# Local attention: one semaphore for the even and one for the odd slots' value transfers

## The reference, cut to what matters

```python
for i in range(DEPTH):            # 6
    x = attn_layer(shift_tokens(x), Wqkv[i], q_scale[i], k_scale[i], Wo[i]) + x
    x = ffn_layer(shift_tokens(x), ln_g[i], ln_b[i], W1[i], b1[i], W2[i], b2[i]) + x
```

```python
bk2, bv2 = (look(bk), look(bv))   # each window with the one before
sim = jnp.einsum('bhwie,bhwje->bhwij', bq, bk2) * QK_SCALE
attn = jax.nn.softmax(jnp.where(mask, -jnp.finfo(sim.dtype).max, sim), -1)
out = jnp.einsum('bhwij,bhwje->bhwie', attn, bv2)
```

## Time and profile before

| what | value |
|---|---|
| three runs | 2665.85, 2668.93, 2667.49 us |
| median | 2667.49 us |
| profiled execution | 2667.58 us |
| its span, first to last instruction | 2665.8 us |
| mean granted TensorE clock | 0.971 of full |
| PE / DVE / ACT / POOL busy | 2491.4 / 2005.2 / 1888.8 / 1764.4 us |
| local stage, first to last attention product | 630.8 to 2309.7 us |

### The profile page before, as it was taken

How to read it: one execution, slowest core, us unless ns; L and a number is a source line. 1 busy time by engine, 2 the same in 40 slices (tenths; PEclk the granted TensorE clock), 3 DMA queues, 4 the chain that set the end, 5 groups by cost and what they waited for, 6 DMA issues and landing times.

```text
span 2665.8 us, 98075 instructions
## 1 busy us (share of the span) xinstructions
PE 2491.4 (93%) x36437; PEld 1732.2 (65%) x36441; DVE 2005.2 (75%) x4387; ACT 1888.8 (71%) x6630; POOL 1764.4 (66%) x1605
## 2 busy tenths in 40 slices
PE   6999788987899999999999999999999999789999
PEld 5888444444666666666666666666666666458884
DVE  5555576766688888888888888888888888565544
ACT  4777666755788888888888878888888888543323
POOL 1777755537788887887888888888887888312210
PEclk9999888888999999999999999999999999989999
DMA  4000100002111211121111111111112111100000
GB/s 117 14 14 15 47 10 9 10 8 80 29 32 35 63 38 35 33 57 40 40 34 52 47 39 33 47 50 42 33 33 64 42 33 33 38 1 1 1 1 16
DMA packets 176292, 91.06 MB, mean 34 GB/s; under 512 B 40926, under 2 KB 172232, under 8 KB 175824
## 3 DMA queue, kind: packets, MB, share of 16 engines
q1 hardware_dynamic: 167200, 80.50, 11.2%
q0 software_dynamic: 8192, 4.21, 1.1%
q10 hardware_dynamic: 432, 0.07, 0.0%
HBM read 30.57 MB, written 3.76 MB: 13 GB/s over the span
## 4 chain that ended last, share of the span: by engine, by line
PE 27%; DMA 23%; SPq 19%; issue 3%; DVE 2%; ACT 0%; DVEq 0%
DMA rg_prod<-vt 22%; SPq L556 18%; PE bank L1119 3%; PE bank L1136 2%; PE scores L1171 2%; PE bank L1182 2%; PE bank L1126 2%; PE scores L1153 1%; PE bank L1852 1%; PE bank L1876 1%; PE bank L2109 1%; PE bank L1846 1%; PE bank L1870 1%; PE bank L1211 1%; PE bank L1108 1%
## 5 line engine op out<-in xcount | busy, mean ns | idle before, releaser
L1554 POOL TENSOR_TENSOR rs<-ssc,neg_half 128x8 f32<-128x8 f32 x384 | 647.2, 1685 | 40.8 <-DVE ssc L1375 40.7
L1482 ACT ACTIVATE pr<-scores,negmax 128x64 f32<-128x64 f32 x1536 | 461.8, 313 | 58.5 <-DVE negmax L1383 32.8
L1544 POOL TENSOR_TENSOR t_pair<-qn_pair,tabs 128x512 f32<-128x512 f32 x384 | 489.1, 1274 | 13.9 <-DVE qn_pair L1363 13.1
L1534 POOL TENSOR_TENSOR pr<-pr,rec 128x256 f32<-128x256 f32 x384 | 235.7, 614 | 305.4 <-DVE rec L1355 304.9
L1119 PE MATMUL bank<-wqk,xs 128*128 128x512 f32 x768 | 405.1, 610 | 22.0 <-DVE qn_pair L1363 19.3
L1013 POOL DMA_INDIRECT rg_win<-rg_images,share_down x256 | 253.6, 991 | 144.4 <-DVE rg_prod L952 89.9
L1482 ACT ACTIVATION_READ_ACCUMULATOR pr<-scores,negmax 128x1 f32 x1536 | 311.6, 203 | 0.0
L1371 DVE TENSOR_REDUCE ss<-sq 128x8 f32<-128x512 f32 x384 | 261.4, 681 | 30.9 <-ACT sq L1505 29.8
L1363 DVE TENSOR_TENSOR qn_pair<-bank,rs 128x512 f32<-128x512 f32 x384 | 258.2, 672 | 29.8 <-POOL rs L1554 29.6
L1473 ACT COPY vt<-bank 128x256 f32<-128x256 f32 x361 | 135.2, 375 | 203.9 <-issue 116.7
L1136 PE MATMUL bank<-oT,wo 128*128 128x128 f32 x1536 | 266.4, 296 | 0.0
(11 more groups left out here) (307 smaller groups left out, 5596.0 us busy)
## 6 DMA issues: line engine op xcount, KB each, us to landing
rg_prod<-vt SPq DMA_DIRECT2D x1536, 32.0 KB
wqk<-in_L_ffn_Wqkv SPq DMA_DIRECT2D x20, 256.0 KB
rg_win<-rg_images,share_down POOLq DMA_INDIRECT x256
wv<-in_L_ffn_Wqkv SPq DMA_DIRECT2D x20, 128.0 KB
wo<-in_L_ffn_Wo SPq DMA_DIRECT2D x20, 128.0 KB
w<-in_L_ffn_W SPq DMA_DIRECT2D x6, 341.0 KB
rg_images<-rg_prod SPq DMA_DIRECT2D x1, 1625.0 KB, 8.0
rg_images<-XT SPq DMA_DIRECT2D x16, 64.0 KB
```

Source lines behind the costliest of these rows:

```text
L1482: ex = act.activation(pr[t % 2][:, h * BAND:(h + 1) * BAND], sl_ps[:, h // 2, h % 2 * BAND:(h % 2 + 1) * BAND], ACT.Exp, bias=negmax[t % 2 ...
L1544: pool.tensor_tensor(t2[t % 2][:, :].rearrange("p (i h f e) -> p i h f e", i=2, h=GH, f=2), qn[t % 2][:, :].rearrange("p (i h f e) -> p i ...
L1554: pool.tensor_tensor(rs[t % 2][:, :], ssc[t % 2][:, :], neg_half[:, 0:8], ALU.pow)\
```

## The change

The single semaphore becomes two. The transfers of even jobs raise the first, those of odd jobs the second. SP's wait at L554 asks for the transfers of job t-2 and is left out for the first two jobs. PE asks for this job's own, by the parity's count. The two copies ask for job t-3's, by that job's parity; ACT has no such wait for the first three jobs. Nothing else is touched.

```diff
-        self.v_spread = sem("attn_v_spread")
+        self.v_spread = [sem(f"attn_v_spread{i}") for i in range(2)]
...
                     sp.wait_ge(a.o_ready, TICKS + t - 1)
-                    if t:
-                        sp.wait_ge(a.v_spread, 64 * t)
+                    if t >= 2:
+                        sp.wait_ge(a.v_spread[t % 2], 64 * (t // 2))
                     for to, half, key, a_pair in ((0, 0, WINDOW, 0), (0, 1, HD, 0), (HD, 0, WINDOW, 1), (HD, 1, 0, 1)):
                         sp.dma_start(far[to:to + HD, half * P:(half + 1) * P],
-                                     near[key:key + BAND, a_pair * P:(a_pair + 1) * P]).then_inc(a.v_spread, 16)
+                                     near[key:key + BAND, a_pair * P:(a_pair + 1) * P]).then_inc(a.v_spread[t % 2], 16)
...
                 pe.wait_ge(a.pT_moved, TICKS + t + 1)
-                pe.wait_ge(a.v_spread, 64 * (t + 1))
+                pe.wait_ge(a.v_spread[t % 2], 64 * (t // 2 + 1))
...
                     dve.wait_ge(a.o_ready, TICKS + t - 2)
-                    dve.wait_ge(a.v_spread, 64 * (t - 2))
+                    dve.wait_ge(a.v_spread[(t - 3) % 2], 64 * ((t - 3) // 2 + 1))
...
                     act.wait_ge(a.o_ready, TICKS + t - 2)
-                    act.wait_ge(a.v_spread, 64 * max(t - 2, 0))
+                    if t >= 3:
+                        act.wait_ge(a.v_spread[(t - 3) % 2], 64 * ((t - 3) // 2 + 1))
```

## The result

| | before | changed |
|---|---|---|
| runs | 2665.85, 2668.93, 2667.49, 2661.22 us | 2644.14, 2636.15, 2639.70, 2642.06 us |
| median | 2666.67 us | 2640.88 us |
| profiled execution, its span | 2667.58, 2665.8 us | 2644.14, 2642.3 us |

The ratio is 0.9913, with a 95% interval of 0.9893 to 0.9933: by the ratio 23 us faster, somewhere between 18 and 29; the medians differ by 25.8. The forecast was 2648.5 us, in a range of 2644.0 to 2658.0. The profiled execution of the changed kernel, 2644.14 us, is the slowest of its four and lies 3.3 us above their median; that of before lies 0.9 above its own. So the two profiles differ by 23.4 us and not by 25.8.

The account below looks back on a forecast made before the run. The prediction took SP's transfer turn, about as slow as TensorE's slot, to bound the local stage. Its terms, 19.1 + 1.6 - 3.9 + 2.5 = 19.3 us, and a count by cycles led to 19.0: 2648.5 us, range 2644 to 2658.

Parts of the forecast that it names:

- Two things at nearly the same pace, and a queue that can't make up what it loses: Local stage: SP's transfer turn averages about 4.3 us against a TensorE slot of 4.31 to 4.38, so attention is held.
- The part by part costs: Waits on PE, DVE and ACT cost nothing; SP's value copy is long done, transfers lead attention by 3 to 4.5 us.
- Given back, 3.9 us: TensorE's waits before the scores, after ACT's three Gelus per chunk, grow from 17.2 to 21.1 us over 22 chunks.
- The last slots, 0.9 and 2.5 us: Stage end: 0.9 us gained for two held slots behind 2253.27, 2.5 us for the last two slots.
- By cycles, 13.1 to 17.5 us: Second count, 19 chunk cycles from 925.00 to 2253.27 us: an excess of 17.5, or 13.1 if 4.4 stay.
- first rival: The ring of engines sets the slot, so stalls return: half back 2658 us, chance 0.12; all back 2663.4.
- the 19.1 us: TensorE's stalls before attention, 750 to 2290 us: 16.2 us idle plus 2.9 for overlap with the scores' bar.
- the first term of the sum: TensorE's idle time before attention from 750 to 2290 us, 16.2 us for 49 held slots, is gained.
- Rival 4: More is gained: nothing of the 3.9 us before the scores comes back, 2644.4 us; chance 0.03.
- my 19.0: Whole kernel: forecast gain of 19.0 us, taken between the two counts, from 2667.5 to 2648.5 us.
- Stalls passed on to other engines: Local stage: other engines needed the rest held attentions gave; half back 2658 us, chance 0.12, all back 2663.4.
- Transfers queuing behind weights: SP's transfers share rings with 60 weight loads; slower if each delays them above 4.3 us, 2678 at 4.4; chance 0.03.

Follow-up runs that it names:

- first pair: The first measurement of the unedited kernel before and the changed kernel, each with its profile: medians 2666.67 and 2640.88 us.
- second pair of the first kind: Later unedited single executions beside each other, images stage at the low clock: kernel before (third profile) 2659.61 us, changed kernel (third profile) 2638.08 us.
- first kind: Executions with a granted clock of 0.86 to 0.88 in the images stage; at first, medians 2666.67 us before and 2640.88 changed.
- second kind: Executions with a granted clock of 0.98 to 1.00 in the images stage; unedited repeat 2579.97 us changed against 2603.05 before.

## Why the prediction was wrong, point by point

- **Two things at nearly the same pace, and a queue that can't make up what it loses.** Right, and shown from both sides: one issue less removes the stalls without a second semaphore, one more costs 185 us with the old wait and nothing with the new.
- **The part by part costs.** The new waits of PE, DVE and ACT cost nothing that shows, as the serial version with two semaphores has it. Of SP two readings were wrong. The value copy is not "long done": SP stood 120.2 us for it, 269 times, 0.45 us each. And the lead was not 3 to 4.5 us in every slot. In the first profile of the changed kernel its median is 3.9, but one job in ten has 2.8 or less, and job 60, beside the weight reload at the first layer's end, has 0.49, where the worst was put at 1.6. It was enough all the same.
- **Given back, 3.9 us.** Right: the wait before the scores, at most 0.96 us a chunk, summed to 20.8 us where 21.1 were forecast.
- **The last slots, 0.9 and 2.5 us.** Too high for the first pair: 2.05 us from chunk 22 to the state update, because waits of 0.31 and 0.77 us for copies on ACT remain. In the second pair of the first kind the same stretch gave 4.0.
- **By cycles, 13.1 to 17.5 us.** Right for the profiles it was made from: 14.5, and 16.4 for the second pair of the first kind (1330.1 against 1313.7). But two of the 19 cycles, from chunk 4 to chunk 6, still take 69.8 to 70.0 us in every profile of the changed kernel, outside the 68.9 to 69.4 that I gave; nothing is held in them.
- **The price of the first rival.** It is inconsistent: with all of the 19.1 us handed back it leaves 4.1, with half of them it also takes off the 3.9. By the first rule half leaves 9.55 + 4.1 = 13.7 us, 2653.8 and not 2658.
- **The step that failed** is the first term of the sum: "Idle time of TensorE before attention from 750 to 2290 us: 16.2 us, for 49 held slots." I read it from one execution and used it as a constant of the kernel. I had written that a turn is about 4.3 us against a slot of 4.31, and did not draw from it that such a difference cannot be known from one profile. In the same window the unchanged kernel had 18.7 us in its second profile of the first kind (22.2 us held instead of 19.0) and 29.7 us in the second kind (33.0 held):

```profile
L1171 PE MATMUL scores<-pT,vt 64*64 64x32 f32 (+1 forms) x2824 | 194.7, 230 | 18.7 <-issue 14.6 <-DMA rg_prod<-vt 2.6
L1171 PE MATMUL scores<-pT,vt 64*64 64x64 f32 (+1 forms) x2744 | 189.2, 230 | 29.7 <-issue 23.3 <-DMA rg_prod<-vt 5.2
```

  Rival 4, my limit for more gain (2644.4), only took back the 3.9 us, so the range had no room for larger stalls. With the second kind's figures in the same sum (28.7 to 33.1 us held, 1.8 to 4.0 for late weights, 1.4 for the last two slots, 5.4 to 7.5 given back) it comes to 27 to 31 us, where the profiles from the first query product to the end show 23 to 27. So there the term alone is large enough. Of the 6.8 us by which the medians of the first kind beat my 19.0, the second profile shows 3.2; the cause of the rest stays open, as said below.
- **The median hid it.** The profiled execution was at the median of the runs, and I used it as if this made each part typical. It did not. Its images stage took longer than that of the other profile of before in the same kind, 300.96 us as shown above, though the work is the same:

```profile
287.17:600.91 313.74, 270.68 (x4096) 139.16 (x4097) 222.34 (x450) 202.12 (x397) 161.65 (x173) 0.86 0.09 17
```

  12.8 us more there, with 89 us at 1.2 GHz instead of 72, and fewer held attentions than in every other profile with the old wait: one hid the other.
- **What stays open.** In the second kind it adds up: from the first query product to the end, the three kernels with the old wait and four transfers take 2072.6 to 2077.3 us, the changed one, the one without a wait and the one with three transfers 2048.1 to 2049.9, some 26 us less, and the medians differ by 23 to 25. In the first kind the same stretch is 14.0 us shorter in one pair of profiles and 20.3 in the other, while the medians differ by 25.8 us and the interval begins at 18. From chunk 3 to the state update the two pairs gained 16.6 and 20.4 us, on either side of the 19.3 of the sum. Whether the executions without a profile had more stalls, or whether the images stage, which took from 299 to 314 us in the four profiles of this kind, happened to favour the changed kernel, no run here tells. The clock is one part of it: over the four runs of the changed kernel the time falls from 2644.14 to 2636.15 us as the mean granted clock rises from 0.967 to 0.973.
- **The rivals.** Stalls passed on to other engines: only some 3.6 of the 3.9 us. By the Trainium skill's rule on weight loads (Perfetto Trace Analysis, Identifying the Most-Contended Engine) TensorE with 68% should have had room; the traces do not agree that another engine was the limit, since in all six profiles with at most three held attentions chunk 3 to 22 took 1313.7 to 1314.6 us and the chain ran through TensorE (68 to 80% of it). Transfers queuing behind weights: the loads did land later, but it cost nothing. In the queue's timeline of the changed kernel, against the earlier trace rows:

```profile
1438.78 0.53 SPq L562 DMA_DIRECT2D wqk<-in_L_ffn_Wqkv  x1
1443.16 0.35 SPq L568 DMA_DIRECT2D wv<-in_L_ffn_Wqkv  x1
```

  SP was blocked for 4.4 us instead of 2.9, near the point of 4.3 from which I had let this rival win, and still no attention was held: the transfers behind it, those of job 188, landed 1.0 us ahead of their use. The rival was nearer than I had it, with 0.49 us left at job 60.

## What to carry to other kernels

A wait on one's own last transfer makes issue and landing one serial turn. Compare that turn with the consumer's slot: where they are within a few per cent, the cost is a small difference of two large numbers, and one profile does not give its size; take several, or give the range the width that a 1% longer turn would make. The cure need not be a second semaphore: one issue less per turn gave the same time here, and with two semaphores SP's wait on its own transfers could be left out, since the one on attention keeps them in order. And that a profiled execution lies at the median says nothing about its parts: compare each stage that the sum rests on with a second profile.

## What the runs showed of the hardware

- TensorE's granted clock in the images stage was 0.86 to 0.88 in some executions and 0.98 to 1.00 in others, for the same work, 299 to 314 us against 240 to 241. In the slower ones the trace has 13 spells at 1.2 GHz, of 3.4 to 10.2 us each and 72 to 89 us in all; in the others at most two, of 10 us in all.
- In the local stage (900 to 2100 us) the granted clock was 1.00 in both kinds, and below it only in the two kernels whose TensorE stood still longest before attention, 141 and 134 us from 750 to 2200: the fifth transfer with the old wait (0.98) and the start one slot later (0.99). In the first of them:

```profile
900.00:2300.00 1400.00, 1244.11 (x21093) 868.65 (x21097) 1068.98 (x2379) 1029.94 (x3920) 1004.56 (x872) 0.98 0.17 44
```

- Issues of these transfers cost 0.48 us for the first of a job and 0.60 for the others, but 151 to 156 of 1536 took over 0.7 in the kernels with the old wait, for 106 to 118 us more in all; in the changed kernel 122 to 134, for 77 to 80. The mean time from the fourth issue's end to the landing also fell, from 1.50 to 1.54 us to 1.38 to 1.41. In the changed kernel most issues start 0.10 us behind an attention's end, before 2.8 to 3.2 us behind it; whether that place makes them cheaper was not tried.
